# A graph kernel's first layer: the node update moved into the pass over the edges, tile by tile

## What is computed

```
h   = relu(layernorm(x))
m   = relu([h[src], h[dst], edge_attr] @ W1.T + b1)        # one row per edge
agg = segment_sum(m @ W2.T + b2, dst)                      # one row per node
u   = relu(agg @ Wu.T + bu)
x1  = x + (layernorm(h + u) * gamma + beta)
h1  = relu(layernorm(x1))                                  # the next layer's input
```

## Time and profile before

| what | value |
|---|---|
| median of the runs | 2386.38 us |
| the profiled execution, its own time | 2400.12 us |
| its span, first to last instruction | 2398.6 us |
| edge pass, first gather to last flag instruction | 142 to 1397 us |
| first tail, first instruction to the first matmul of layer 2 | 1404.8 to 1491.7 us |
| TensorE, VectorE, ScalarE, GpSimd busy over the span | 65%, 40%, 27%, 38% |
| mean granted clock of TensorE | 0.74 of full speed |

### The profile page before, as it was taken

One profiled execution on the slowest core, in us unless ns is written; L12 is line 12 of the kernel. 1 busy time (PEld: TensorE's weight loads), 2 busy tenths in 40 slices (PEclk: granted clock), 3 DMA queues, 4 the chain that ended last, 5 costly groups with the idle time before them and its releaser, 6 DMA issues. The chain is left out here.

```text
span 2398.6 us, 31354 instructions
## 1 busy us (share of the span) xinstructions
PE 1557.9 (65%) x10942; PEld 1012.2 (42%) x10942; DVE 957.5 (40%) x2738; ACT 659.2 (27%) x1639; POOL 900.3 (38%) x911
## 2 busy tenths in 40 slices
PE   1405555555555555555455553998978989599997
PEld 1303333434333333334333342675645556445544
DVE  5644454545445454545455446221322124301111
ACT  1303333333333333334333311121323332100000
POOL 5046666666666666666666622000000000000001
PEclk8655666665556666666666655998889989799999
DMA  6423434343443434343343432000100001594571
GB/s 160 119 62 101 119 104 124 109 125 106 112 119 103 124 109 125 107 121 109 106 123 107 121 111 59 1 1 8 41 15 2 5 9 33 191 332 174 200 270 60
DMA packets 203234, 247.43 MB, mean 103 GB/s; under 512 B 36541, under 2 KB 177416, under 8 KB 203061
## 3 DMA queue, kind: packets, MB, share of 16 engines
q1 hardware_dynamic: 174260, 184.35, 24.3%
q0 software_dynamic: 28800, 60.80, 9.7%
HBM read 174.04 MB, written 57.60 MB: 97 GB/s over the span
## 5 line engine op out<-in xcount | busy, mean ns | idle before, releaser
L809 POOL DMA_INDIRECT arena<-dram_PHL,src_of x806 | 823.8, 1022 | 495.0 <-issue 213.2
L1026 PE MATMUL psum<-arena 128*128 128x100 f16 x1568 | 220.9, 247 | 260.0 <-issue 215.0
L1026 PEld LDWEIGHTS psum<-arena 128*128 128x128 f16 x1568 | 174.7, 129 | 392.5 <-issue 370.5
L1010 PE MATMUL psum<-arena 128*128 128x128 f16 x1612 | 209.0, 288 | 180.7 <-issue 146.5
L961 ACT ACTIVATE arena<-psum 128x512 f16<-128x512 f32 x202 | 120.5, 596 | 649.5 <-remote 574.2
L1028 PE MATMUL psum<-arena 128*128 128x50 f16 x1568 | 213.3, 229 | 57.0 <-issue 56.5
L1010 PEld LDWEIGHTS psum<-arena 128*128 128x128 f16 x1612 | 147.6, 130 | 216.4 <-issue 215.8
L2275 POOL DMA_DIRECT2D parts_a<-dram_x x7 | 5.3, 763 | 609.1 <-POOLq L2473 586.0
L880 DVE SCALAR_TENSOR_TENSOR agg_all<-psum,agg_all 128x64 f32<-128x64 f32 x202 | 44.5, 221 | 403.2 <-remote 399.4
L1028 PEld LDWEIGHTS psum<-arena 128*128 128x128 f16 x1568 | 171.5, 114 | 71.1 <-issue 69.8
L869 DVE SCALAR_TENSOR_TENSOR arena<-psum,arena 128x512 f16<-128x512 f32 x202 | 138.4, 685 | 151.7 <-issue 103.8
(11 more groups left out here) (359 smaller groups left out, 2135.3 us busy)
## 6 DMA issues: line engine op xcount, KB each, us to landing
arena<-dram_aw SPq DMA_DIRECT2D x7, 6400.0 KB, 20.4
dram_aw<-arena SPq DMA_DIRECT2D x196, 200.0 KB
arena<-dram_aw SPq DMA_DIRECT2D x3, 4800.0 KB, 17.1
arena<-in_ea_quads SPq DMA_DIRECT2D x51, 256.0 KB
arena<-dram_rel SPq DMA_DIRECT2D x51, 256.0 KB
arena<-arena SPq DMA_DIRECT2D x408, 32.0 KB
arena<-dram_PHL,src_of POOLq DMA_INDIRECT x806
arena<-dram_aw SPq DMA_DIRECT2D x2, 4000.0 KB, 14.8
```

The costliest lines, as they stand in the source:

```text
L809: nc.gpsimd.indirect_dma_start(gathered_p[:, slot, k, :], None, d["PHL"], bass.IndirectOffsetOnAxis(ap=src_of[:, b:b + 1], axis=0)).then_i ...
L1010: nc.tensor.matmul(out[:, k * P:(k + 1) * P], side[:, s, at:at + P], node_side[:, g % NAB, part * D:(part + 1) * D], start=(part == 0 and ...
L1026: nc.tensor.matmul(out, hot_lo[:, u, p, :], hot_key[:, u, p, 0:2].rearrange("p a k -> p (a k)"), start=True, stop=False)
```

## The change

The phase `first_tail` no longer runs on this input: it is kept, under a branch on the crowded flag, as `crowded_tail`. Its work is done in `edge_pass`, one tile of 128 nodes at a time. A tile t is due at the step `whole_at(t)` that follows the last group that touches it; its nine pieces stand one step apart, each behind the engine's own work of that step: the product on TensorE in step due+1, `update` on VectorE in due+2, the root on ScalarE in due+3, `residual` in due+4, the second root in due+5, `normalise` and the stores and loads of SyncE in due+6, the high half in due+7 and the low half in due+8. The loop runs over 202 + 9 steps instead of 203. Gamma, beta and the residual, which GpSimd did, are VectorE's now. Two concessions make room: the sums of a group have one bank of PSUM where they had two (so `sum_up(g)` waits for `add(g-1)`, not `add(g-2)`), and there are five gather slots instead of six. The output of the tile goes to `h_first`, a part of the arena, where layer 2 reads it.

```diff
-    NS, NPRE, NPG, NAB = 3, 2, 6, 8
+    NS, NPRE, NPG, NAB = 3, 2, 5, 8
...
-            return psum[:, 6 + g % 2, 0:BAND]
+            return psum[:, 6, 0:BAND]
+
+        def whole_at(t):
+            past = EDGE + (t + 1) * P
+            return 1 + max(g for g in range(MG) if base_of(g) + EDGE < past)
+
+        due = {}
+        for t in range(NT):
+            due[whole_at(t)] = due.get(whole_at(t), []) + [t]
+        LAST = 9
+
+        def tiles_due(step, behind):
+            return due.get(step - behind, [])
+
...
+                def load_nodes(t):
+                    k = t % 2
+                    if t < 2:
+                        sp.wait_ge(folded, 1)
+                    else:
+                        sp.wait_ge(y_varied, t - 1)
+                        sp.wait_ge(v_given, t - 1)
+                        sp.wait_ge(x_stored[k], 16 * (t // 2))
+                    sp.dma_start(h0[:, k], d["h0"][nodes_of(t), :]).then_inc(node_in[k], 16)
+                    sp.dma_start(x[:, k], d["x"][nodes_of(t), :]).then_inc(node_in[k], 16)
+
+                def store_nodes(t):
+                    sp.wait_ge(x_ready, t + 1)
+                    sp.dma_start(d["x1"][nodes_of(t), :], x[:, t % 2]).then_inc(x_stored[t % 2], 16)
+
...
+                load_tail_weights()
+                for s in range(MG + LAST):
+                    for t in tiles_due(s, 6):
+                        store_nodes(t)
+                        if t + 2 < NT:
+                            load_nodes(t + 2)
+                    if s == 4:
+                        load_nodes(0)
+                        load_nodes(1)
+                    if s > MG:
+                        continue
...
-                for q in range(4):
-                    if q == 0:
-                        sp.wait_ge(added, MG)
-                    n = NPAD // 4
-                    sp.dma_start(d["agg"][:, q * n:(q + 1) * n], agg[:, EDGE + q * n:EDGE + (q + 1) * n]).then_inc(
-                        agg_stored, 16)
...
+                def update(t):
+                    k = t % 2
+                    dve.wait_ge(fold_read, 2)
+                    step(nc.vector.scalar_tensor_tensor(out=y[:, :], in0=b2u[:, :], scalar=deg_of[:, t:t + 1],
+                                                        in1=bu[:, :], op0=ALU.mult, op1=ALU.add))
+                    dve.wait_ge(u_psum, t + 1)
+                    step(nc.vector.tensor_tensor(y[:, :], psum[:, 7, 0:D], y[:, :], ALU.add))
+                    dve.sem_inc(u_read, 1)
+                    dve.wait_ge(node_in[k], 32 * (t // 2 + 1))
+                    step(nc.vector.scalar_tensor_tensor(out=y[:, :], in0=y[:, :], scalar=0.0, in1=h0[:, k], op0=ALU.max,
+                                                        op1=ALU.add))
+                    step(nc.vector.bn_stats(y_stats[:, :], y[:, :]))
+                    nc.vector.bn_aggr(y_mv[:, :], y_stats[:, :]).then_inc(y_varied, 1)
+
+                def residual(t):
+                    k = t % 2
+                    dve.wait_ge(y_rooted, t + 1)
+                    step(nc.vector.reciprocal(y_std[:, :], y_std[:, :]))
+                    step(nc.vector.tensor_scalar(y[:, :], y[:, :], y_mv[:, 0:1], y_std[:, 0:1], ALU.subtract, ALU.mult))
+                    step(nc.vector.tensor_tensor(y[:, :], y[:, :], gamma[:, :], ALU.mult))
+                    step(nc.vector.tensor_tensor(y[:, :], y[:, :], beta[:, :], ALU.add))
+                    step(nc.vector.tensor_tensor(x[:, k], x[:, k], y[:, :], ALU.add))
+                    dve.sem_inc(x_ready, 1)
+                    step(nc.vector.bn_stats(x_stats[:, :], x[:, k]))
+                    nc.vector.bn_aggr(x_mv[:, :], x_stats[:, :]).then_inc(x_varied, 1)
+
+                def normalise(t):
+                    dve.wait_ge(x_rooted, t + 1)
+                    step(nc.vector.reciprocal(x_std[:, :], x_std[:, :]))
+                    nc.vector.tensor_scalar(v[:, :], x[:, t % 2], x_mv[:, 0:1], x_std[:, 0:1], ALU.subtract, ALU.mult
+                                            ).then_inc(v_given, 1)
+
+                def low_of_tile(t):
+                    dve.wait_ge(hi_parts, t + 1)
+                    nc.vector.tensor_tensor(parts.of(1, t), v[:, :], parts.of(0, t), ALU.subtract
+                                            ).then_inc(lo_parts_made, 1)
+
...
-                for s in range(MG + 1):
+                for s in range(MG + LAST):
                     if s + 1 < MG:
                         hots(s + 1)
                     if s + 1 < J:
                         pair_hots(s + 1)
                     if s < MG:
                         low_parts(s)
-                    if s >= 1:
...
+                    for t in tiles_due(s, 8):
+                        low_of_tile(t)
+                    for t in tiles_due(s, 6):
+                        normalise(t)
+                    for t in tiles_due(s, 4):
+                        residual(t)
+                    for t in tiles_due(s, 2):
+                        update(t)
...
+                def root_y(t):
+                    act.wait_ge(y_varied, t + 1)
+                    nc.scalar.activation(y_std[:, :], y_mv[:, 1:2], ACT.Sqrt, bias=d["eps"][:, 0:1]).then_inc(y_rooted, 1)
+
+                def root_x(t):
+                    act.wait_ge(x_varied, t + 1)
+                    nc.scalar.activation(x_std[:, :], x_mv[:, 1:2], ACT.Sqrt, bias=d["eps"][:, 0:1]).then_inc(x_rooted, 1)
+
+                def high_of_tile(t):
+                    act.wait_ge(v_given, t + 1)
+                    nc.scalar.activation(v[:, :], v[:, :], ACT.Relu, scale=parts.up).then_inc(v_relued, 1)
+                    act.wait_ge(v_relued, t + 1)
+                    nc.scalar.copy(parts.of(0, t), v[:, :]).then_inc(hi_parts, 1)
+
...
+                    for t in tiles_due(s, 7):
+                        high_of_tile(t)
+                    for t in tiles_due(s, 5):
+                        root_x(t)
+                    for t in tiles_due(s, 3):
+                        root_y(t)
...
-                    if g >= 2:
-                        pe.wait_ge(added, g - 1)
+                    if g:
+                        pe.wait_ge(added, g)
...
+                def update_product(t):
+                    pe.wait_ge(added, whole_at(t))
+                    if t:
+                        pe.wait_ge(u_read, t)
+                    else:
+                        pe.wait_ge(fold_read, 2)
+                        pe.wait_ge(degrees_read, 1)
+                    at = slice(EDGE + t * P, EDGE + (t + 1) * P)
+                    nc.tensor.matmul(psum[:, 7, 0:D], agg[:, at], w2u[:, :], start=True, stop=True).then_inc(u_psum, 1)
...
+                    for t in tiles_due(s, 1):
+                        update_product(t)
...
-def first_tail(nc, new, d):
+def crowded_tail(nc, new, d):
...
+                with pool.If(d["crowded"]["Pool"] >= 1):
...
-        flow = [(first_tail, (), Parts(a, D)),
-                (wide_layer, (), Parts(b, M2, d["scale_y"][:, 0:1], d["scale_y"][:, 1:2])),
+        d["h_out"] = d["h_first"]
+        crowded_tail(nc, new, d)
+        end_phase()
+        d["h_in"] = d["h_first"]
+        flow = [(wide_layer, (), Parts(b, M2, d["scale_y"][:, 0:1], d["scale_y"][:, 1:2])),
```

More of the change, by code:

```diff
@@ L72 @@
 H1, M2 = 2 * D, 48
+H_FIRST = NT * NCOL - NT * 2 * D
 LN_EPS = 1e-5
@@ L889, in ea_low, with step, spread_b2 @@
                                                    op0=ALU.mult, op1=ALU.subtract).then_inc(lo_done, 1)
+                steps = [0]
+                def step(ins):
+                    steps[0] += 1
+                    ins.then_inc(dve_step, 1)
+                    dve.wait_ge(dve_step, steps[0])
+                def spread_b2():
+                    dve.wait_ge(tail_w_in, 16 * 6)
+                    nc.vector.tensor_scalar(b2_wide[:, :], d["ones"][:, :], b2[:, 0:1], None, ALU.mult
+                                            ).then_inc(b2_spread, 1)
@@ new lines, in degrees @@
+                def degrees():
+                    dve.wait_ge(fold_read, 2)
+                    sums = psum[:, 7, 2 * D:2 * D + 2 * NT].rearrange("p (q t) -> p q t", q=2)
+                    nc.vector.tensor_copy(deg_of[:, :], sums[:, 1])
+                    step(nc.vector.tensor_scalar(d["eps_deg"][:, :], sums[:, 1], 1.0, None, ALU.max))
+                    step(nc.vector.tensor_scalar(wsum[:, :], sums[:, 0], 1.0, None, ALU.add))
+                    dve.sem_inc(degrees_read, 1)
+                    nc.vector.reciprocal(d["inv_deg"][:, :], d["eps_deg"][:, :])
+                    step(nc.vector.tensor_scalar(positive[:, :], wsum[:, :], 0.0, None, ALU.is_gt))
+                    nc.vector.tensor_scalar(d["eps_deg"][:, :], d["eps_deg"][:, :], L2_EPS, None, ALU.mult)
+                    nc.vector.tensor_scalar(wsum[:, :], wsum[:, :], 1e-38, None, ALU.max).then_inc(wsum_ready, 1)
@@ L911, in _ @@
                         ea_low(s // QUAD + 2)
-                steps = [0]
-                def step(ins):
```

(11 more changed lines are left out.)

353 lines of the change are left out of this document (200 added, 153 removed).

## The result

The changed kernel takes 2320.4 us (median of 4 runs, 2318.8 to 2321.9) where the kernel before took 2385.9: a ratio of 0.9725, with a 95% interval of 0.9708 to 0.9742. The profiled execution took 2320.96 us, span 2319.4, so it stands for the median. That of the kernel before did not (2400.1 against 2386), so I compare with a second profile of it as well, which took 2385.85.

What follows compares the result with a forecast made beforehand. The prediction took a chain of waits, not one full engine, to bound the kernel. From a median of 2386.4 us, 74.6 go and 62 come into the edge pass: 2374 us, range 2330 to 2440.

Steps and rivals of the forecast that it cites:

- What goes: Between the last `add` and layer 2: 98.1 us shrink to 23.5 of drain, flag, barriers and skipped phases, so 74.6 go.
- What bounds the kernel: Steady edge pass: no engine is full at 6.1 us a step, so a chain of waits sets the pace.
- VectorE, 39 us: Edge pass: of 108 us of tile work moved to VectorE, 39 lengthen the pass, between 25 and 108.
- the cheapest rival: Edge pass: 25 us on VectorE or less and little else, 2330 to 2345 us; chance 0.14.
- One bank, 6 us: Edge pass: `sum_up` also waits for the `add` of the group before, costing 6 us.
- its rival: Edge pass: with one bank TensorE stands still while `add` is late, 50 us more, 2424 us; chance 0.22.
- The start, 4 us: Start: weights, folding and degrees, 8 more queue issues and some 12 small operations, cost 4 us, between 0 and 10.
- Five slots: 0: Edge pass: a gather slot less still leaves GpSimd four groups ahead, costing 0 us.
- TensorE 5, ScalarE 2, SyncE 6: Edge pass: us added by the tiles' products on TensorE, short operations on ScalarE, and transfers and store waits on SyncE.
- The rule against the change: Edge pass: VectorE's fp32 operations beside GpSimd take 0.678 instead of 0.342 us, or gathers wait as long: 76 us more.
- nearly everything hides: Edge pass: VectorE's moved work costs 25 us or less and little else, since no engine is full; 2330 to 2345, chance 0.14.
- GpSimd becomes the bound: Edge pass: the lock or the missing slot adds 0.3 us a gather, 80 less slack, about 2430 us; chance 0.03.

## Why the prediction was wrong

**What goes** was right: 73.7 us where 74.6 were forecast. Its terms were drain 10.1 (11.6 forecast), flag 3.7 (3.5), barriers and skipped phases 10.6 (8.4).

**What bounds the kernel** is the step that failed. "None is full [...] So a chain of waits sets the pace and not one engine" took GpSimd's 154 us of waits for a slot as slack, and VectorE's 331 us before `add` as a wait that some piece on VectorE could lengthen. The rows already had a hint against it: these waits were ended by "remote", not by TensorE's matmuls. The runs put in its place: the pace hangs on the number of gathers (half of them take the step from 6.14 to 5.10, and to 4.29 with the loads split). Four gathers take GpSimd 5.1 us, and with all of them under way TensorE's signals come late (75 `add`s late by over 2 us, 3 or none with half of them), to GpSimd's own wait for a slot too. VectorE's waits lie in between, and neither leaving its work out nor doubling it moved the step by more than 0.09.

**VectorE, 39 us**, came out at about 8, and at most some 13. Its work itself was sized well, 4.06 us a tile where 4.31 were forecast. The step that failed in it is the floor: "the queue behind `hots` [...] is late by the whole piece: 25 us count in full". The chain over the loads, the stores and ScalarE is real, but with all gathers it does not set the pace: taking some 2.5 us a quad out of ScalarE's wait for the store changed nothing. That a delay of it ends in the same wait for a late signal is my reading of the timeline; no run delays that chain alone. Since I took 25 as nearly certain, even the cheapest rival stopped at 2330, and the range with it; with nothing at all for the moved work the sum would have been 2386.4 - 74.6 = 2311.8.

**One bank, 6 us**: 0.0002 of the time, 0.6 us, with an interval of -2.4 to 3.3. In the changed kernel TensorE does wait 35 us in 1000 for `add` before `sum_up`, and its rival was wrong that this would cost 50 us: the single part cost nothing that a measurement shows, and the whole change 4 to 12 with all its terms. **The start, 4 us**: it gained about 6, since the burst of gathers that holds all engines up is shorter by one slot. "Five slots: 0" was right for the steady step only. **TensorE 5, ScalarE 2, SyncE 6**: not measured one by one; with all the rest the pass lost 6 us, of which -6 are the start and 0 to 8 VectorE, so together they cost some 4 to 12. That is as small as what two profiles differ by, so it shows the size and no more.

**The rule against the change** did not show. VectorE did 79 us more work in 1000, most of it fp32, and with the doubled work 55 more still in the 800 us from 400 to 1200 (512 after 457). The gathers took 1009 and 996 ns, where they took 1025; in the changed kernel the 103 that ran beside an operation of the tiles took 993 ns on average. VectorE's scaling kept its 0.35 us beside gathers. The Trainium skill (SBUF — State Buffer, "SBUF: two separate sides") says that while VectorE runs an operation in a mode with two ports, such as a copy of fp32 within SBUF, GpSimd is locked out of the ports that they share and can't write the descriptors of its DMAs. No row here tells the mode of an operation, and none has a gather made longer. The 678 ns of the earlier trace rows is a mean of two kinds: single scalings took up to 1.42 us beside GpSimd's additions and 0.34 without one, and the pass has none of these additions.

Of the rivals, "nearly everything hides" had the right outcome with too high a floor; its reason, that no engine is full, is not what the runs showed. "GpSimd becomes the bound" named the engine; most of the step was its time already, and neither VectorE's work nor the missing slot made it worse.

## What to carry to other kernels

When every engine is part idle and the waits are ended by signals later than any visible work, look for what is common to them before adding up a chain; here one cut of a suspect (half the gathers) told more than all sums over the timeline. Here work put on an engine that waited in this way was nearly free, and a shortcut in the chain around it gained nothing. Price a term that "counts in full" with a lower end as well, and profile the kernel before twice when its profiled execution is off its median.

## What was not expected of the hardware

While indirect gathers follow each other on GpSimd, TensorE's signals to the other engines come late, and at the start of the pass its instructions too. There one matmul was started in 1.4 to 2.1 us instead of one in 0.05, for 14 us, and the others went on about 4 us after the start of the last of 24 gathers. In the steady pass `add` waited until 779.86 for 0.6 us of matmuls begun at 770.92. Rows of 256 B instead of 512 changed nothing, iotas of the same length on GpSimd don't do it, and neither does a TensorE that stands still, as the kernel with half the gathers shows. Which part of a gather does it (its descriptors, its completion signals, or its count of rows) stays open: no run here separates these. That TensorE's slow stretches don't set the pace is shown by the runs with fewer matmuls and with the loads split; that the late signals reach GpSimd's own wait and so close the loop is read from the timeline, and only the 0.86 us a step are measured.
